# Feed-forward stage of a post-norm transformer layer: the factors of both norms computed in common instructions, second norm's sum and statistics, the low part of x and the output projection in new places

## The chip, the cores and the metric

The kernel runs on one core of one Trainium2 chip. The metric is the device time of one execution in microseconds. The core has five engines that run their own instruction streams in order and meet at semaphores: TensorE (PE, matmuls and transposes; PEld is its weight load), VectorE (DVE), ScalarE (ACT), GpSimd (POOL) and SyncE (SP, which issues the transfers here). A wait at the head of an engine's stream holds everything behind it.

## The reference

8 sequences of 1024 tokens, 256 features, 16 heads of 16, feed-forward width 704, all in float32. A layer is attention, a layer norm over the residual, a feed-forward block whose two linear layers quantize both operands blockwise to a 4-bit grid, and a second layer norm:

```python
def _layernorm(x, axis=-1, eps=1e-05):
    m = jnp.mean(x, axis=axis, keepdims=True)
    v = jnp.var(x, axis=axis, keepdims=True)
    return (x - m) / jnp.sqrt(v + eps)

def fp4_quant_dequant(x):                     # blocks of 16 along the last dim
    xb = x.reshape(shape[:-1] + (shape[-1] // BLOCK, BLOCK))
    scale = jnp.max(jnp.abs(xb), axis=-1, keepdims=True) / 6.0
    scale = jnp.maximum(scale, jnp.float32(1e-12))
    xn = xb / scale
    idx = jnp.searchsorted(_MID, jnp.abs(xn))
    return (_GRID[idx] * jnp.sign(xn) * scale).reshape(shape)

def fp4_linear(x, w):
    return jnp.einsum('bsk,nk->bsn', fp4_quant_dequant(x), fp4_quant_dequant(w))

# attention: softmax(q k^T / 4) v for 16 heads, output projection with scale and bias
x = _layernorm(x + attention(x))              # first norm
h = silu(fp4_linear(x, w_gate)) * fp4_linear(x, w_up)
x = _layernorm(x + fp4_linear(h, w_down))     # second norm
```

## The kernel before

The program has three stages. The first two project q, k and v and compute attention; they end about 1470 us into the profiled execution. The third, `feed`, does everything from the output projection to the second norm. It handles the 8192 tokens as 64 tiles of 128 tokens (tokens on the partitions, features along them) in a software pipeline: in step i each engine does one piece of work for each of several tiles. Tile i-1 is projected and its first norm computed; tile i-2 has x quantized; tile i-3 goes through the gate and up products and silu; tile i-4 has h quantized; tile i-5 has h transposed; tile i-6 goes through the down product; tile i-7 gets residual sum and second norm's statistics; tile i-8 is normalized and stored. The number in the code that goes with each piece is this lag. Steps 1 and 2, and part of step 3, lie inside the attention stage; the steps run to 71. The order of the pieces within a step is written out by hand for each engine, and every hand-over is a semaphore whose count is the tile's number (`due`).

What one step does, engine by engine, with the lines of the profile:

- VectorE: block maxima of h (L1482, 128x44 out) and of x (L1482, 128x16), low part of the transposed x (L1517), the block scales of both in one instruction (L1466) and their reciprocals (L1472), division of x and of h (L1488, 256 and 704 wide), the residual sum y after the output projection (L1537) and its statistics (L1541, L1548), the sum that rounds x (L1495, 256 wide) and the difference that brings it back (L1552), the residual sum z after the down product (L1557), its statistics (L1563, L1573), the sum that rounds h (L1495, 704 wide), and the product silu(gate) * up (L1568).
- GpSimd: the factor of the first norm, (variance + eps) ** -0.5, in two instructions of one column (L1579 the sum, L1580 the power); x's grid value times its scale (L1601); h's difference `hg` (L1608); h's grid value times its scale `hq` (L1613); the factor of the second norm, again L1579 and L1580. In steps 54 to 63 two more instructions at the step's start finish the attention output of that tile (L1589, L1591), because from tile 54 on it is loaded raw.
- ScalarE: copy of the transposed x (L1446), the output (L1375 and L1376 make the bias from mean and factor, L1384 applies both), the two bends of x (L1416, L1420) and of h (L1426, L1430), silu (L1399), three copies of the transposed h (L1407, L1408, L1411), and the first norm (L1375, L1376, L1392).
- TensorE: transposes of x (L1354), output projection (L1286), down product (L1337, whose last, half-height chunk L1345 is done for two tiles at once in every second step), gate and up product (L1298), transposes of h (L1309). In the first step after attention the projection stands ahead of the transposes of x.

The second norm's factor of a step is the last work of that step on GpSimd; the output that ScalarE makes from it is the second piece of the next step. In that next step ScalarE's bends of h (L1426, L1430) stand behind the output, and VectorE's h-rounding sum waits for the second of them (`hm_ready`).

Of the kernel before, what the change touches and what calls it, by code (L numbers as in the profile page):

```python
# [12 lines left out]
ALU = mybir.AluOpType  # L13
# [3 lines left out]
P = 128  # L17
BANK = 512
NB, S, H = 8, 1024, 256
# [1150 lines left out]
def feed(nc, sem, room, first_room, buffers, x_tok, ctx_dram, rden_dram, out_tok, ps, ident, wT, s_all, b_row, wguT, wd, wdT,  # L1170
# [3 lines left out]
    NT = T // P  # L1174
# [9 lines left out]
    def takes(room):  # L1184
# [4 lines left out]
        def take(*shape):  # L1189
# [21 lines left out]
    h = take(I)  # L1211
    hn = take(2, I)
    z = take(2, H)
    names = ("xb_ready ctx_ready wo_psum wo_used mv1_ready rstd1_ready "
             "x1_ready xsum_ready xgrid_ready xq_ready xt_psum xqT_high xqT_ready xn_ready xm_ready xbend_ready hn_ready hm_ready hbend_ready gate_psum up_psum silu_ready h_made "
             "hsum_ready hgrid_ready hq_ready hT_psum hT_ready dn_read dn_psum z_used mv2_ready rstd2_ready fin_ready "
             "stats1_ready stats2_ready grid_chain pow1_chain pow2_chain shift1_chain shift2_chain").split()
    sems = {name: sem(name) for name in names}
    stored = [sem(f"stored{j}") for j in range(2)]

# [6 lines left out]

    def each(ks):
        return (At(None, k, U) for k in ks)

    def sync(sp, ks):
        def load(t):
# [43 lines left out]
    def tensor(pe, ks, cs=range(HC)):  # L1276
# [79 lines left out]
            last.then_inc(sems["xt_psum"], 1)  # L1356

        for i in each(ks):
            order = ((3, x1_by_width), (1, output_projection), (6, down), (3, gate_and_up), (5, h_by_width))
            if i.k == FILL:  # L1360

                pe.wait_ge(wt_split, 2 * HC)
                order = (order[1], order[0]) + order[2:]
            for lag, stage in order:
                if lag == 6 and 0 <= i.k - FILL < IC // 2:
                    wd_across(i.k - FILL)
                if i.plus(-lag).ok(NT):
                    stage(i.plus(-lag))

    def scalar(act, ks, lags=range(9)):  # L1370
# [6 lines left out]
            link.close()  # L1377

        def output(t):
            due(act, "rstd2_ready", t.lin(1, 1))  # L1380
            shift(t, 1, "shift2_chain")

            wait(act, stored[t.slot(2)], t.turn(2, 16))
            nc.scalar.activation(fin[:, t.slot(2)], z[:, t.slot(2)], ACT.Identity, bias=centre[:, 1, 1:2],  # L1384
                                 scale=rstd[:, 1, 1:2]).then_inc(sems["fin_ready"], 1)

        def x1_normal(t):
            due(act, "rstd1_ready", t.lin(1, 1))
            shift(t, 0, "shift1_chain")

            due(act, "z_used", t.lin(1, 1 - U))
            nc.scalar.activation(x1[:, t.slot(U)], y[:, :], ACT.Identity, bias=centre[:, 0, 1:2],  # L1392
                                 scale=rstd[:, 0, 1:2]).then_inc(sems["x1_ready"], 1)
# [53 lines left out]
                                 ACT.Copy).then_inc(sems["xqT_high"], 1)  # L1447

        for i in each(ks):
            for lag, stage in ((3, copy_xqT), (8, output), (2, bend_x), (4, bend_h), (3, silu), (5, copy_hT),  # L1450
                               (1, x1_normal)):
                if lag in lags and i.plus(-lag).ok(NT):
                    stage(i.plus(-lag))
                if lag == 3 and stage is copy_xqT and 0 <= i.k - FILL < IC // 2:
                    copy_wd(i.k - FILL)

    def vector(dve, ks):
# [39 lines left out]
        for i in each(ks):  # L1497
# [12 lines left out]
            if on2:  # L1510
                due(dve, "x1_ready", t2.lin(1, 1))

                due(dve, "xq_ready", t2.lin(1, -1))
                gx.top()
            if on3:
# [4 lines left out]
            if on2 or on4:  # L1520
                which = slice(0 if on4 else NBH, NBH + NBX if on2 else NBH)
                tops, scales, inverses = (blocks[:, i.slot(2), n, which] for n in range(3))
                scale(tops, scales)
                invert(scales, inverses)
            if on2:
                gx.divide().then_inc(sems["xn_ready"], 1)
            if on4:
                gh.divide().then_inc(sems["hn_ready"], 1)
            if on1:
# [7 lines left out]
                nc.vector.scalar_tensor_tensor(out=y[:, :], in0=ps[:, WO, 0:H], scalar=s_all[:, 3:4],  # L1537
                                               in1=pairs[:, pair % PAIRS, 1, half], op0=ALU.mult,
                                               op1=ALU.add).then_inc(sems["wo_used"], 1)
                due(dve, "wo_used", t1.lin(1, 1))  # L1540
                nc.vector.bn_stats(stats[:, 0], y[:, :]).then_inc(sems["stats1_ready"], 1)  # L1541
            if on2:
                gx.add("xm_ready").then_inc(sems["xsum_ready"], 1)
            if on1:

                due(dve, "stats1_ready", t1.lin(1, 1))
                due(dve, "rstd1_ready", t1.lin(1))
                nc.vector.bn_aggr(mv[:, 0], stats[:, 0]).then_inc(sems["mv1_ready"], 1)  # L1548
            if on2:
                due(dve, "xsum_ready", t2.lin(1, 1))  # L1550
                due(dve, "xq_ready", t2.lin(1))
                nc.vector.tensor_tensor(xg[:, :], xn[:, :], xm[:, :],  # L1552
                                        ALU.subtract).then_inc(sems["xgrid_ready"], 1)
            if on7:
                due(dve, "dn_psum", t7.lin(1, 1))
                due(dve, "fin_ready", t7.lin(1, -1))
                nc.vector.tensor_tensor(z[:, t7.slot(2)], ps[:, DN[t7.slot(2)], 0:H], x1[:, t7.slot(U)],  # L1557
                                        ALU.add).then_inc(sems["z_used"], 1)
            if on4:
                gh.add("hm_ready").then_inc(sems["hsum_ready"], 1)  # L1560
            if on7:
                due(dve, "z_used", t7.lin(1, 1))
                nc.vector.bn_stats(stats[:, 1], z[:, t7.slot(2)]).then_inc(sems["stats2_ready"], 1)  # L1563
# [5 lines left out]
            if on7:  # L1569

                due(dve, "stats2_ready", t7.lin(1, 1))
                due(dve, "fin_ready", t7.lin(1))
                nc.vector.bn_aggr(mv[:, 1], stats[:, 1]).then_inc(sems["mv2_ready"], 1)  # L1573

    def gpsimd(pool, ks):
        def power(t, n, chain, name):

            link = Chain(pool, sems[chain], 1, t)
            link(nc.gpsimd.tensor_tensor(rstd[:, n, 0:1], mv[:, n, 1:2], numbers[:, 0:1], ALU.add))  # L1579
            nc.gpsimd.tensor_tensor(rstd[:, n, 1:2], rstd[:, n, 0:1], numbers[:, 1:2],  # L1580
                                    ALU.pow).then_inc(sems[name], 1)
            link.close()

        for i in each(ks):
            if RAW <= i.k < NT:
# [6 lines left out]
            t = i.plus(-1)  # L1592
            if t.ok(NT):
                due(pool, "mv1_ready", t.lin(1, 1))
                due(pool, "x1_ready", t.lin(1))
                power(t, 0, "pow1_chain", "rstd1_ready")
# [21 lines left out]
            if t.ok(NT):  # L1618
# [30 lines left out]
```

## Time and profile before

| | |
|---|---|
| time, median of 3 runs (lowest to highest) | 2056.46 us (2052.69 to 2057.95) |
| time of the profiled execution | 2051.83 us |
| its span | 2050.0 us |
| PE busy | 1987.0 us (97%) |
| DVE busy | 1881.0 us (92%) |
| ACT busy | 1674.6 us (82%) |
| POOL busy | 751.6 us (37%) |
| granted TensorE clock | nine tenths or more of full speed in all 40 slices |
| chain that ended last, by engine | PE 68%, POOL 13%, issue 7%, ACT 7%, DVE 4% |

The span is what the profiler saw of the instructions; 1.8 us lie around it. Busy shares are of the whole span, and about seven tenths of it are projections and attention, which the change leaves as they are. In the chain of waits the shares of POOL come from the lines of `feed` (L1613 and L1608 4% each, L1580 3%, L1601 2%, L1579 1%). A view of a few steps of `feed` says more than any share: the timeline by instruction, in which the same pattern repeats every step.

### The profile page before, as it was taken

The numbers are of one execution on the slowest core, as the hardware profiler recorded it, in microseconds if no ns is written. First come the engines' busy times: TensorE is split into PE (matmuls) and PEld (weight loads), VectorE is DVE, ScalarE is ACT, GpSimd is POOL, SyncE is SP. The second block draws the span as 40 slices with busy tenths as digits, with TensorE's granted clock in tenths as the row PEclk, the third lists the DMA queues.
The fourth block names the chain that finished last, engine by engine and source line by source line (L and its number), as shares of the span: only waits on it lengthen the run. The fifth ranks groups of instructions, "written<-read, shape, count | busy, mean of one in ns | idle before, by whom it ended". The sixth has DMA issues, their size and how long they took to land.

```text
span 2050.0 us, 42089 instructions
## 1 busy us (share of the span) xinstructions
PE 1987.0 (97%) x15806; PEld 1044.0 (51%) x15806; DVE 1881.0 (92%) x2345; ACT 1674.6 (82%) x3244; POOL 751.6 (37%) x749
## 2 busy tenths in 40 slices
PE   8999999999999999999999999999999999999997
PEld 7766333333333333333333333334477777777775
DVE  4788999999999999999999999997399999999996
ACT  6656888888888888888889888888877777777775
POOL 3000446665764561100010010000155555555784
PEclk9999999999999999999999999999999999999999
DMA  7885632444354354435435444542111111111210
GB/s 234 273 248 200 110 51 45 79 96 91 75 100 93 78 95 90 90 82 103 89 71 101 91 84 88 97 91 75 43 40 47 47 40 42 47 47 52 62 32 21
DMA packets 119000, 181.40 MB, mean 88 GB/s; under 512 B 29644, under 2 KB 74444, under 8 KB 118796
## 3 DMA queue, kind: packets, MB, share of 16 engines
q1 hardware_dynamic: 111116, 171.10, 36.2%
q10 hardware_dynamic: 7392, 7.34, 1.1%
q8 instruction: 125, 2.05, 0.5%
q14 instruction: 79, 0.65, 0.1%
q0 software_dynamic: 288, 0.27, 0.1%
HBM read 103.68 MB, written 73.40 MB: 86 GB/s over the span
## 4 chain that ended last, share of the span: by engine, by line
PE 68%; POOL 13%; issue 7%; ACT 7%; DVE 4%; DMA 1%; POOLq 0%; SPq 0%; DVEq 0%
PE ps L913 29%; PE ps L966 28%; POOL hq L1613 4%; PE ps L494 4%; POOL hg L1608 4%; POOL rstd L1580 3%; PE ps L504 3%; ACT craw L1033 2%; PE ps L935 2%; POOL fq L1601 2%; POOL rstd L1579 1%; ACT xm L1420 1%; ACT bend_of_x L1416 1%; PE ps L481 1%; ACT centre L1376 1%
## 5 line engine op out<-in xcount | busy, mean ns | idle before, releaser
L1079 DVE TENSOR_REDUCE negmax<-ps 128x1 f32<-128x1024 f32 x980 | 1182.5, 1219 | 19.7 <-PE ps L913 14.1
L1025 ACT ACTIVATE room<-ps 128x512 f32<-128x512 f32 x2048 | 1102.8, 599 | 118.3 <-PE ps L935 86.7
L935 PE MATMUL ps<-qs,ks 50*128 50x512 f32 x2048 | 745.6, 449 | 1.9 <-ACT room L1025 1.0
L913 PE MATMUL ps<-ks,qs 48*128 48x512 f32 x1960 | 714.5, 444 | 0.0
L966 PE MATMUL ps<-room,vals 128*17 128x256 f32 x8192 | 637.3, 385 | 8.9 <-ACT craw L1033 0.2
L913 PEld LDWEIGHTS ps<-ks,qs 48*128 48x128 f32 x1960 | 288.6, 184 | 414.3 <-DVE negmax L1079 333.0
L164 POOL CAST mrow<-turned_rows 128x32 fp32r<-128x32 f32 x32 | 6.7, 210 | 904.3 <-DVE turned_rows L159 690.8
L966 PEld LDWEIGHTS ps<-room,vals 128*17 128x17 f32 x8192 | 140.0, 95 | 371.4 <-issue 209.5
L935 PEld LDWEIGHTS ps<-qs,ks 50*128 50x128 f32 x2048 | 304.2, 184 | 18.2 <-ACT room L1025 14.3
L1298 PE MATMUL ps<-wguT,xqT 128*128 128x512 f32 (+1 forms) x1152 | 266.8, 384 | 1.4 <-DVE xqT L1517 1.4
L1298 PEld LDWEIGHTS ps<-wguT,xqT 128*128 128x128 f32 x1152 | 210.8, 188 | 48.9 <-issue 9.6
L1337 PE MATMUL ps<-wdT,hT 128*128 128x256 f32 x640 | 150.6, 382 | 5.0 <-ACT hT L1408 5.0
L1136 POOL TENSOR_SCALAR fq<-fq 88x1024 f32<-88x1024 f32 (+1 forms) x42 | 137.5, 3274 | 3.6
L1375 ACT ACTIVATE centre<-mv 128x1 f32<-128x1 f32 x128 | 25.5, 199 | 132.5 <-POOL rstd L1580 132.3
L1337 PEld LDWEIGHTS ps<-wdT,hT 128*128 128x128 f32 x640 | 122.1, 192 | 22.8 <-issue 5.6
L1608 POOL TENSOR_TENSOR hg<-room,hm 128x704 f32<-128x704 f32 x64 | 97.7, 1526 | 45.7 <-DVE room L1495 45.7
L1579 POOL TENSOR_TENSOR rstd<-mv,numbers 128x1 f32<-128x1 f32 x128 | 33.9, 265 | 202.1 <-DVE mv L1548 195.2
L1495 DVE TENSOR_TENSOR room<-room,hm 128x704 f32<-128x704 f32 x64 | 75.6, 1181 | 22.2 <-ACT hm L1430 21.8
L569 ACT ACTIVATE qf<-ps,b_col,s_all 128x512 f32<-128x512 f32 x64 | 49.9, 780 | 52.9 <-PE ps L494 50.0
L1613 POOL TENSOR_TENSOR hq<-hg,blocks 128x704 f32<-128x704 f32 x64 | 88.8, 1388 | 5.0
L494 PE MATMUL ps<-qs,wqk 128*128 128x512 f32 x256 | 80.4, 436 | 0.0
L1138 POOL TENSOR_TENSOR fq<-fq 88x1024 f32<-88x1024 f32 (+1 forms) x36 | 77.3, 2148 | 2.6
(111 smaller groups left out, 2154.3 us busy)
## 6 DMA issues: line engine op xcount, KB each, us to landing
qk_parts<-parts SPq DMA_DIRECT2D x64, 512.0 KB, 3.9
qs<-qk_parts SPq DMA_DIRECT2D x192, 128.0 KB, 4.5
ks<-qk_parts SPq DMA_DIRECT2D x192, 128.0 KB, 7.1
ctx_raw<-craw SPq DMA_DIRECT2D x64, 256.0 KB
ready<-passing SPq DMA_DIRECT2D x27, 512.0 KB, 6.6
pairs<-ready SPq DMA_DIRECT2D x27, 512.0 KB
out_dram<-fin SPq DMA_DIRECT2D x64, 128.0 KB, 1.7
xin<-in_L_attn_x_dram ACTq DMA_DIRECT2D x14, 512.0 KB, 5.5
```

The costliest lines, as they stand in the source:

```text
L494: last = nc.tensor.matmul(ps[:, QK + m % 2, :], wqk[:, a, m // 2, c, (m % 2) * P:(m % 2 + 1) * P], x_half[:, i.slot(2), c, :], start=n == ...
L913: return nc.tensor.matmul(ps[:, MX + 2 * (item[i.k, u] % 2) + bank, :], qs[rows, i.slot(RING), pair, t * P:(t + 1) * P], ks[rows, i.slot(R ...
L935: nc.tensor.matmul(ps[:, score_bank(i, s, n), :], ks[rows, slot, pair, kt * P:(kt + 1) * P], qs[rows, slot, pair, qh * BANK:(qh + 1) * BAN ...
L966: last = nc.tensor.matmul(ps[h * AV:h * AV + DV, PV, cols], vals[:, i.k // NG * KT + kt, i.k % NG * GH + h, :], prob[:, prob_slot(i, s), h ...
L1025: nc.scalar.activation(prob[:, prob_slot(i, s), score_order(i, s)[n], :], ps[:, score_bank(i, s, n), :], ACT.Exp, scale=float(D) ** -0.5). ...
L1079: nc.vector.tensor_reduce(negmax[:, j.slot(RING), max_column(u):max_column(u) + 1], ps[:, bank:bank + 2, :], AX.XY, ALU.max, negate=True). ...
L1136: link(nc.gpsimd.tensor_scalar(dst, norm, mid * mid, gain, ALU.is_gt, ALU.mult))
L1138: link(nc.gpsimd.tensor_tensor(mag, mag, tmp, ALU.add))
L1298: last = nc.tensor.matmul(ps[:, GU + n0 // BANK, 0:n1 - n0], xqT[:, a, c, :], wguT[:, b, c, n0:n1], start=n == 0 and c == 0, stop=n == len ...
L1337: last = nc.tensor.matmul(ps[:, DN[t.slot(2)], 0:H], hT[:, c, :], wdT[:, c, :], start=c == 4, stop=False)
L1608: nc.gpsimd.tensor_tensor(hg[:, :], hn[:, t.slot(2)], hm[:, t.slot(2)], ALU.subtract).then_inc(sems["hgrid_ready"], 1)
L1613: nc.gpsimd.tensor_tensor(hq[:, :].rearrange("p (n e) -> p n e", e=BLK), hg[:, :].rearrange("p (n e) -> p n e", e=BLK), hs[:, t.slot(2), 1 ...
```

## The change

All edits are in `feed`.

1. GpSimd computes the factors of both norms in common instructions of two columns (one of each norm, 128x2), in steps where both norms have a tile; the pair of one-column instructions behind `hq` is gone, and the common pair stands between x's grid value (now first in the step) and h's difference `hg`. It waits for the statistics of both norms. One semaphore, `rstd_ready`, counts the steps in place of one for each norm.
2. VectorE: the block scales and reciprocals stand ahead of the low part of x; the second norm's sum z, statistics and their aggregate stand earlier, between h's division and the first norm's work; the rounding and difference of x stand ahead of y. The first norm's aggregate is last before h's rounding sum.
3. ScalarE: the first norm stands ahead of the copies of the transposed h.
4. TensorE: the output projection stands ahead of the transposes of x in every step.

```diff
 # scalar
-            due(act, "rstd2_ready", t.lin(1, 1))
+            act.wait_ge(sems["rstd_ready"], factors(t.plus(7)))      # output
...
-            due(act, "rstd1_ready", t.lin(1, 1))
+            act.wait_ge(sems["rstd_ready"], factors(t.plus(1)))      # x1_normal
...
-            for lag, stage in ((3, copy_xqT), (8, output), (2, bend_x), (4, bend_h), (3, silu), (5, copy_hT),
-                               (1, x1_normal)):
+            for lag, stage in ((3, copy_xqT), (8, output), (2, bend_x), (4, bend_h), (3, silu), (1, x1_normal),
+                               (5, copy_hT)):
 # tensor
-            order = ((3, x1_by_width), (1, output_projection), (6, down), (3, gate_and_up), (5, h_by_width))
...
+            for lag, stage in ((1, output_projection), (3, x1_by_width), (6, down), (3, gate_and_up), (5, h_by_width)):
 # gpsimd
-        def power(t, n, chain, name):
...
+        def power(i, norms):
...
+            nc.gpsimd.tensor_tensor(rstd[:, norms, 0], mv[:, norms, 1],
+                                    numbers[:, 0:1].to_broadcast([P, norms.stop - norms.start]),
+                                    ALU.add).then_inc(sems["pow_chain"], 1)
+            pool.wait_ge(sems["pow_chain"], i.k)
+            nc.gpsimd.tensor_tensor(rstd[:, norms, 1], rstd[:, norms, 0],
+                                    numbers[:, 1:2].to_broadcast([P, norms.stop - norms.start]),
+                                    ALU.pow).then_inc(sems["rstd_ready"], 1)
...
+            t1, t7 = i.plus(-1), i.plus(-7)
+            if t1.ok(NT):
+                due(pool, "mv1_ready", t1.lin(1, 1))
+                due(pool, "x1_ready", t1.lin(1))
+            if t7.ok(NT):
+                due(pool, "mv2_ready", t7.lin(1, 1))
+                due(pool, "fin_ready", t7.lin(1))
+            if t1.ok(NT) or t7.ok(NT):
+                power(i, slice(0 if t1.ok(NT) else 1, 2 if t7.ok(NT) else 1))
             t = i.plus(-4)
...
-            t = i.plus(-7)
-            if t.ok(NT):
-                due(pool, "mv2_ready", t.lin(1, 1))
-                due(pool, "fin_ready", t.lin(1))
-                power(t, 1, "pow2_chain", "rstd2_ready")
```

`factors(i)` is the number of the step, `i.k`, which is what `rstd_ready` has counted once that step's power is done.

VectorE's order in a step of the steady part, before, from the block scales to h's rounding sum (`room` holds h, hn and z, `fq` holds y, x1, xn and xg):

```order
L1466 SCALAR_TENSOR_TENSOR blocks<-blocks,numbers 128x60
L1472 RECIPROCAL blocks<-blocks 128x60
L1488 SCALAR_TENSOR_TENSOR fq<-fq,blocks 128x256
L1488 SCALAR_TENSOR_TENSOR room<-room,blocks 128x704
L1537 SCALAR_TENSOR_TENSOR fq<-ps,s_all,pairs 128x256
L1541 BN_STATS stats<-fq 128x6
L1495 TENSOR_TENSOR fq<-fq,xm 128x256
L1548 BN_AGGR mv<-stats 128x2
L1552 TENSOR_TENSOR fq<-fq,xm 128x256
L1557 TENSOR_TENSOR room<-ps,fq 128x256
L1495 TENSOR_TENSOR room<-room,hm 128x704
```

The same place in the changed kernel, from the low part of x to h's rounding sum (its lines are other numbers: L1526 is the low part of x, L1492 the divisions, L1536 z, L1499 the rounding sums, L1556 y):

```order
L1526 TENSOR_TENSOR xqT<-ps,xqT 128x256
L1492 SCALAR_TENSOR_TENSOR fq<-fq,blocks 128x256
L1492 SCALAR_TENSOR_TENSOR room<-room,blocks 128x704
L1536 TENSOR_TENSOR room<-ps,fq 128x256
L1499 TENSOR_TENSOR fq<-fq,xm 128x256
L1542 BN_STATS stats<-room 128x6
L1546 TENSOR_TENSOR fq<-fq,xm 128x256
L1556 SCALAR_TENSOR_TENSOR fq<-ps,s_all,pairs 128x256
L1563 BN_AGGR mv<-stats 128x2
L1566 BN_STATS stats<-fq 128x6
L1570 BN_AGGR mv<-stats 128x2
L1499 TENSOR_TENSOR room<-room,hm 128x704
```

The low part of x came from ahead of the scales to behind the reciprocals, the statistics of z came from behind h's rounding sum to ahead of it, and the first norm's aggregate went from the middle to the last place before that sum.

GpSimd's order, before, one step from the first norm's factor to the second norm's:

```order
L1579 TENSOR_TENSOR rstd<-mv,numbers 128x1
L1580 TENSOR_TENSOR rstd<-rstd,numbers 128x1
L1601 TENSOR_TENSOR fq<-fq,blocks 128x256
L1608 TENSOR_TENSOR hg<-room,hm 128x704
L1613 TENSOR_TENSOR hq<-hg,blocks 128x704
L1579 TENSOR_TENSOR rstd<-mv,numbers 128x1
L1580 TENSOR_TENSOR rstd<-rstd,numbers 128x1
```

And in the changed kernel, one step:

```order
L1603 TENSOR_TENSOR fq<-fq,blocks 128x256
L1583 TENSOR_TENSOR rstd<-mv,numbers 128x2
L1587 TENSOR_TENSOR rstd<-rstd,numbers 128x2
L1619 TENSOR_TENSOR hg<-room,hm 128x704
L1624 TENSOR_TENSOR hq<-hg,blocks 128x704
```

Four small instructions became two with two columns, and they stand right ahead of h's difference; nothing is behind `hq` in the step any more.

## Rows read from the trace of the kernel before

**Rows 1.** Waits, 1480 to 1950 us: who waited for whom, total, times, longest.

```profile
ACT centre L1375 <- POOL rstd L1580: 102.2, 50, 2.2
...
DVE room L1495 <- ACT hm L1430: 17.4, 48, 0.4
```

**Rows 2.** Timeline of one step: start, duration, instruction, idle before and its releaser.

```profile
1708.88 1.30 DVE L1495 TENSOR_TENSOR room<-room,hm 128x704 f32<-128x704 f32 x1 [0.38 <-ACT hm L1430]
...
1710.26 1.53 POOL L1608 TENSOR_TENSOR hg<-room,hm 128x704 f32<-128x704 f32 x1 [0.82 <-DVE room L1495]
...
1711.87 1.39 POOL L1613 TENSOR_TENSOR hq<-hg,blocks 128x704 f32<-128x704 f32 x1
...
1713.21 0.19 POOL L1579 TENSOR_TENSOR rstd<-mv,numbers 128x1 f32<-128x1 f32 x1
...
1713.48 0.55 POOL L1580 TENSOR_TENSOR rstd<-rstd,numbers 128x1 f32<-128x1 f32 x1
...
1714.07 0.20 ACT L1375 ACTIVATE centre<-mv 128x1 f32<-128x1 f32 x1 [2.18 <-POOL rstd L1580]
...
1714.65 0.60 ACT L1384 ACTIVATE fin<-room,centre,rstd 128x256 f32<-128x256 f32 x1
...
1716.01 0.78 ACT L1426 ACTIVATE bend_of_h<-room 128x704 f32<-128x704 f32 x1
...
1717.73 1.30 DVE L1495 TENSOR_TENSOR room<-room,hm 128x704 f32<-128x704 f32 x1 [0.38 <-ACT hm L1430]
```

**Rows 3.** Timeline, VectorE in the same step, from the product to the divisions.

```profile
1710.44 0.86 DVE L1568 TENSOR_TENSOR room<-room,ps 128x704 f32<-128x704 f32 x1
...
1711.34 0.89 DVE L1482 TENSOR_REDUCE blocks<-room 128x44 f32<-128x704 f32 x1
...
1712.14 0.41 DVE L1482 TENSOR_REDUCE blocks<-fq 128x16 f32<-128x256 f32 x1
1712.47 0.41 DVE L1517 TENSOR_TENSOR xqT<-ps,xqT 128x256 fp32r<-128x256 f32 x1
1712.80 0.53 DVE L1466 SCALAR_TENSOR_TENSOR blocks<-blocks,numbers 128x60 f32<-128x60 f32 x1
...
1713.37 0.53 DVE L1472 RECIPROCAL blocks<-blocks 128x60 f32<-128x60 f32 x1
...
1713.93 0.42 DVE L1488 SCALAR_TENSOR_TENSOR fq<-fq,blocks 128x256 f32<-128x256 f32 x1
...
1714.27 0.88 DVE L1488 SCALAR_TENSOR_TENSOR room<-room,blocks 128x704 f32<-128x704 f32 x1
```

**Rows 4.** Timeline, the end of the same step on VectorE and GpSimd.

```profile
1715.08 0.48 DVE L1537 SCALAR_TENSOR_TENSOR fq<-ps,s_all,pairs 128x256 f32<-128x256 f32 x1
...
1716.47 0.17 DVE L1548 BATCH_NORM_AGGREGATE mv<-stats 128x2 f32<-128x6 f32 x1
1716.59 0.42 DVE L1552 TENSOR_TENSOR fq<-fq,xm 128x256 f32<-128x256 f32 x1
1716.73 0.34 POOL L1579 TENSOR_TENSOR rstd<-mv,numbers 128x1 f32<-128x1 f32 x1 [2.69 <-DVE mv L1548]
...
1717.66 0.62 POOL L1601 TENSOR_TENSOR fq<-fq,blocks 128x256 f32<-128x256 f32 x1
```

**Rows 5.** Timeline, h's rounding sum in two steps without a second norm.

```profile
1489.63 0.89 DVE L1495 TENSOR_TENSOR room<-room,hm 128x704 f32<-128x704 f32 x1 [0.18 <-ACT hm L1430]
...
1497.68 0.89 DVE L1495 TENSOR_TENSOR room<-room,hm 128x704 f32<-128x704 f32 x1 [0.19 <-ACT hm L1430]
```

**Rows 6.** Timeline, a step of the raw tiles: GpSimd's extra work beside h's division.

```profile
1960.98 0.94 POOL L1589 TENSOR_TENSOR pairs<-pairs 128x256 f32<-128x256 f32 x1
...
1961.25 1.42 DVE L1488 SCALAR_TENSOR_TENSOR room<-room,blocks 128x704 f32<-128x704 f32 x1
...
1961.88 1.40 POOL L1591 TENSOR_TENSOR pairs<-pairs,b_row 128x256 f32<-128x256 f32 x1
```

**Rows 7.** Windows: busy PE, PEld, DVE, ACT, POOL (x instructions), clock, DMA share, GB/s.

```profile
1700.00:1800.00 100.00, 94.41 (x479) 78.23 (x478) 93.51 (x192) 73.34 (x174) 58.04 (x80) 1.00 0.15 47
```

More of the change, by code:

```diff
@@ L1213, in feed @@
     z = take(2, H)
-    names = ("xb_ready ctx_ready wo_psum wo_used mv1_ready rstd1_ready "
+    names = ("xb_ready ctx_ready wo_psum wo_used mv1_ready rstd_ready "
              "x1_ready xsum_ready xgrid_ready xq_ready xt_psum xqT_high xqT_ready xn_ready xm_ready xbend_ready hn_ready hm_ready hbend_ready gate_psum up_psum silu_ready h_made "
-             "hsum_ready hgrid_ready hq_ready hT_psum hT_ready dn_read dn_psum z_used mv2_ready rstd2_ready fin_ready "
-             "stats1_ready stats2_ready grid_chain pow1_chain pow2_chain shift1_chain shift2_chain").split()
+             "hsum_ready hgrid_ready hq_ready hT_psum hT_ready dn_read dn_psum z_used mv2_ready fin_ready "
+             "stats1_ready stats2_ready grid_chain pow_chain shift1_chain shift2_chain").split()
     sems = {name: sem(name) for name in names}
@@ L1229, in each, with factors @@
         return (At(None, k, U) for k in ks)
+    def factors(i):
+        return i.k
     def sync(sp, ks):
@@ L1358, in tensor @@
         for i in each(ks):
-            order = ((3, x1_by_width), (1, output_projection), (6, down), (3, gate_and_up), (5, h_by_width))
             if i.k == FILL:
                 pe.wait_ge(wt_split, 2 * HC)
-                order = (order[1], order[0]) + order[2:]
-            for lag, stage in order:
+            for lag, stage in ((1, output_projection), (3, x1_by_width), (6, down), (3, gate_and_up), (5, h_by_width)):
                 if lag == 6 and 0 <= i.k - FILL < IC // 2:
@@ L1514, in vector @@
                 gx.top()
+            if on2 or on4:
+                which = slice(0 if on4 else NBH, NBH + NBX if on2 else NBH)
+                tops, scales, inverses = (blocks[:, i.slot(2), n, which] for n in range(3))
+                scale(tops, scales)
+                invert(scales, inverses)
             if on3:
@@ L1519, in vector @@
                                         ALU.subtract).then_inc(sems["xqT_ready"], 1)
[L1520 to L1524, printed above, removed]
             if on2:
@@ L1528, in vector @@
                 gh.divide().then_inc(sems["hn_ready"], 1)
+            if on7:
+                due(dve, "dn_psum", t7.lin(1, 1))
+                due(dve, "fin_ready", t7.lin(1, -1))
+                nc.vector.tensor_tensor(z[:, t7.slot(2)], ps[:, DN[t7.slot(2)], 0:H], x1[:, t7.slot(U)],
+                                        ALU.add).then_inc(sems["z_used"], 1)
+            if on2:
+                gx.add("xm_ready").then_inc(sems["xsum_ready"], 1)
+            if on7:
+                due(dve, "z_used", t7.lin(1, 1))
+                nc.vector.bn_stats(stats[:, 1], z[:, t7.slot(2)]).then_inc(sems["stats2_ready"], 1)
+            if on2:
+                due(dve, "xsum_ready", t2.lin(1, 1))
+                due(dve, "xq_ready", t2.lin(1))
+                nc.vector.tensor_tensor(xg[:, :], xn[:, :], xm[:, :],
+                                        ALU.subtract).then_inc(sems["xgrid_ready"], 1)
             if on1:
@@ L1539, in vector @@
                                                op1=ALU.add).then_inc(sems["wo_used"], 1)
+            if on7:
+                due(dve, "stats2_ready", t7.lin(1, 1))
+                due(dve, "fin_ready", t7.lin(1))
+                nc.vector.bn_aggr(mv[:, 1], stats[:, 1]).then_inc(sems["mv2_ready"], 1)
+            if on1:
                 due(dve, "wo_used", t1.lin(1, 1))
                 nc.vector.bn_stats(stats[:, 0], y[:, :]).then_inc(sems["stats1_ready"], 1)
-            if on2:
-                gx.add("xm_ready").then_inc(sems["xsum_ready"], 1)
-            if on1:
                 due(dve, "stats1_ready", t1.lin(1, 1))
-                due(dve, "rstd1_ready", t1.lin(1))
+                wait(dve, sems["rstd_ready"], factors(i.plus(-1)))
                 nc.vector.bn_aggr(mv[:, 0], stats[:, 0]).then_inc(sems["mv1_ready"], 1)
[L1549 to L1558, printed above, removed]
             if on4:
                 gh.add("hm_ready").then_inc(sems["hsum_ready"], 1)
-            if on7:
-                due(dve, "z_used", t7.lin(1, 1))
-                nc.vector.bn_stats(stats[:, 1], z[:, t7.slot(2)]).then_inc(sems["stats2_ready"], 1)
             if on3:
@@ L1568, in vector @@
                 nc.vector.tensor_tensor(h[:, :], sg[:, :], up, ALU.mult).then_inc(sems["h_made"], 1)
[L1569 to L1573, printed above, removed]
     def gpsimd(pool, ks):
-        def power(t, n, chain, name):
[L1578 to L1582, printed above, removed]
+        def power(i, norms):
[6 more added lines that the diff above has]
+                                    ALU.pow).then_inc(sems["rstd_ready"], 1)
         for i in each(ks):
@@ L1591, in gpsimd @@
                 nc.gpsimd.tensor_tensor(with_b, with_b, b_row[:, 1], ALU.add).then_inc(sems["xb_ready"], 1)
-            t = i.plus(-1)
-            if t.ok(NT):
-                due(pool, "mv1_ready", t.lin(1, 1))
-                due(pool, "x1_ready", t.lin(1))
-                power(t, 0, "pow1_chain", "rstd1_ready")
             t = i.plus(-2)
@@ L1616, in gpsimd @@
                                         ALU.mult).then_inc(sems["hq_ready"], 1)
-            t = i.plus(-7)
-            if t.ok(NT):
-                due(pool, "mv2_ready", t.lin(1, 1))
-                due(pool, "fin_ready", t.lin(1))
-                power(t, 1, "pow2_chain", "rstd2_ready")
     return Programs(sync, gpsimd, tensor, scalar, vector)
```

## The prediction

> **What bounds the kernel now.** I read the page first, then the waits of ScalarE, VectorE and TensorE in the steady part of `feed`, then the timeline of one step, and last short pieces where a step is different (the first steps, and the raw tiles). The page's busy shares point at TensorE and VectorE, and the shares of its chain at TensorE, but most of the span is attention, so neither says what a step of `feed` is waiting for. The waits do: ScalarE stands idle for 102.2 us in 50 steps, up to 2.2 us each, ahead of L1375 for the power L1580, and VectorE stands idle 0.4 us ahead of L1495 for ScalarE's `hm` in 48 steps [rows 1].
>
> In the timeline these two are parts of one loop that closes after one step [rows 2]. Start to start: h's rounding sum on VectorE to `hg` 1.38, `hg` to `hq` 1.61, `hq` to the second norm's factor 1.34, its two instructions and the hand-over to ScalarE 0.86 (0.27 and 0.59), the bias and the output, then the bends of x up to the first bend of h 1.94 (0.58 and 1.36), that bend and `hm` to the next rounding sum 1.72. Together 8.85 us, and 1708.88 to 1717.73 is 8.85. Nothing in it depends on the output itself; the bends of h only stand behind it in ScalarE's stream. So the second norm's factor sets the step, and the change takes it away from there. The question is what the next loop is, and how long.
>
> **The next loop in the old kernel.** Steps without a second norm show it: rounding sum to rounding sum is 8.05 there [rows 5]. Its links can be read in the steady step. VectorE's block scales L1466 start at 1712.80 and end at 1713.33, just after `hq` ends at 1713.26 [rows 2, 3]. No semaphore ties them; the two engines exclude each other. The same is seen at the other places where a VectorE instruction with two inputs in SBUF meets a GpSimd instruction: the rounding sum takes 1.30 beside x's grid value (1717.66 to 1718.28) and 0.89 where it is alone [rows 2, 4, 5]; the factor's sum L1579 takes 0.34 beside x's difference and 0.19 alone, and ends 0.06 after the other [rows 2, 4]; h's division takes 1.42 in place of 0.88 beside L1589 [rows 3, 6]. The loser ends its own length less some 0.14 after the holder. So `hq` holds back the scales, these the reciprocals, these the divisions, these the bends, and these the rounding sum, whose result makes the next `hg`.
>
> **The change, part by part.**
>
> *Second factor out from behind `hq`.* The loop of 8.85 is cut: the output in the next step finds its factor long done. ScalarE's idle 2.2 us go.
>
> *Common factors ahead of `hg`.* They wait for the first norm's aggregate, and that now starts 0.12 ahead of the rounding sum, which is what an aggregate takes from VectorE's stream (1716.47 to 1716.59). GpSimd follows an aggregate's start after 0.26 [rows 4], so 0.14 after the rounding sum has begun, and by the rows above it is held until that ends. In us after the rounding sum's start: sum of the factor ends at 0.89 + 0.06 = 0.95; power starts at 1.03 (0.08 behind, as 1713.40 to 1713.48) and ends at 1.58; `hg`, which no longer waits for anything else, starts 0.05 before that end, as L1579 does behind `hq`, at 1.53 [rows 2]. Queued behind this wait are `hg`, `hq` and everything that hangs on them. Against 1.38 now this adds 0.15.
>
> *The power on two columns.* No row shows it. The power on one column takes 0.55 where the sum on the same shape takes 0.19 [rows 2]. If the difference of 0.36 is paid once, the second column costs nothing; if it is paid for each column, it costs 0.36 a step. The trace can't say which; I take the middle, 0.18, and keep both ends. Below nothing it cannot go, as the work of one column is in it. The Trainium skill (GPSIMD Engine Reference, Elementwise, side-by-side cycle accounting) gives about 2.6 cycles an element at 1.2 GHz; by that a second column would be 2 ns, and the sum below would lose its whole term for it. That page speaks of ordinary arithmetic, and the power's 0.36 us for one element a partition is far off that rate, so no run here shows what it does for a second.
>
> *VectorE's order.* I space its instructions as the rows do: the next starts 0.08 before the end if independent, 0.03 after it if it reads the result [rows 3]. From `hq` to the reciprocals 1.50 as now (1711.87 to 1713.37), if the scales still lose to `hq`. Then the low part of x in between, 0.45, to x's division 0.33, to h's division 0.34. That is 1.12 where there was 0.90 (1713.37 to 1714.27). From h's division on, up to the rounding sum: 0.81 to z, 0.34 to x's rounding sum, 0.34 to z's statistics, 0.33 to x's difference, 0.34 to y, 0.40 to the second aggregate, 0.11 to the first statistics, 0.46 to the first aggregate (it reads them), 0.12. Together 3.25 (0.42 for the 256-wide instructions, 0.48 for y, from rows 3 and 4). ScalarE would have `hm` ready after 0.96 + 1.72 = 2.68 [rows 2, 3], so VectorE itself closes the loop, and all that was moved ahead of the rounding sum counts in full.
>
> *The new loop.* 1.53 + 1.61 + 1.50 + 1.12 + 3.25 = 9.01 with a free second column, 9.19 with 0.18. It is longer than the 8.85 that it replaces.
>
> *Do the scales still lose?* They follow x's block maxima, and those now wait for x1. From the power's end: 0.04 to ScalarE, 0.23 and 0.35 for the bias, 0.60 for x1, 0.03, 0.44 for the maxima: 1.69. `hq` starts 0.05 before that end plus 1.61: at 1.56. So the scales come 0.13 us late and wait for the whole of `hq`. The power's length moves both alike.
>
> *Moves that cost nothing by themselves.* The copies of the transposed h now follow x1 and come late, some 3.9 us after the rounding sum, and the down product behind them. The projection that now stands ahead of the transposes fills that wait. TensorE is busy 94.41 of 100 us [rows 7], so its own work is 0.944 x 8.85 = 8.35 a step, and below 9.0 it has room; h's product may wait for the up product, and is then up to 0.7 us late, but between it and the end of `hq` VectorE has more slack than that. If that cover is gone, it is the term of the second rival.
>
> *Raw tiles, 10 steps.* GpSimd's two extra instructions now come right behind `hq`, where VectorE has scales and divisions. L1591 holds x's division back by about 0.33: it ends near 1.36 after `hq`, the division would have begun at 0.89 and ends 0.28 after the holder. In the old kernel the like delay (1.42 for 0.88) was covered by ScalarE's output [rows 6].
>
> **Sum.** Steps 8 to 53: 46 x (9.01 - 8.85) = 7.4. Raw steps: 10 x (0.16 + 0.33) = 4.9. First steps without second norm: without z and its statistics VectorE needs some 0.2 less, 8.8 against 8.05, three times: 2.2. Last steps without x: a loop about 0.3 shorter than now, two or three times: -0.7. Second column: 58 x 0.18 = 10.4. Together 24, so 2051.8 + 24 = 2076 for a profiled execution. The median shown is 4.6 above the profiled one; by it, 2080. I say 2079.
>
> **Rivals.**
>
> *A, the port falls the other way and the factors cost nothing* (chance 0.20). If GpSimd's small instructions run beside the rounding sum, `hg` starts at about 0.97 with a free column or 1.10 with 0.18; the loop is 8.45 or 8.58, close to TensorE's own 8.35. 46 x -0.27 = -12, raw steps about 0, ends +1: 2040 to 2046. For it: the removed wait is real, 2 us a step. Against it: L1579 is held by just such an instruction in every step [rows 4].
>
> *B, the scales slip in between `hg` and `hq`* (0.12). The margin is 0.13 us. Then `hq` starts some 0.1 late and x's division waits for its end: 1.71 + 1.71 + 1.39 + 0.20 + 3.25 = 8.26. But then the down product behind the late copies, with its tail in every second step, delays h's product by more than 1 us, and the scales miss in the step after. Half the steps 8.35 to 8.5 and half 9.19 give about 8.85: no gain, raw steps +3: 2051 to 2060.
>
> *C, the second column costs a full 0.36 or more* is the upper end of the forecast: 14 + 21 = 35, so 2087 to 2092.
>
> **How the numbers follow.** Forecast 0.68, A 0.20, B 0.12. A change below 0.3% (6 us) cannot be told from none here; so faster 0.20, same 0.12, slower 0.68. The likeliest case has 2066 (free column) to 2092 (0.36) as its own range. For 8 in 10 I take 2048 to 2096: above to a column somewhat dearer than 0.36, below through B and the nearer edge of A.
>
> **What the new profile would show.** ScalarE's wait ahead of L1375 for the power behind `hq` is gone, and it now waits ahead of the first norm. The factor's sum on two columns takes about 0.75, ending just after the rounding sum's end; `hg` starts 1.5 to 1.9 after the rounding sum's start. VectorE shows no wait for `hm`; the scales take over 1 us, ending with `hq`. Rounding sums come 9.0 to 9.4 apart. I am wrong if the factor's sum takes 0.2 and `hg` starts within 1.2 (A), or if the scales take 0.3 in many steps (B), or if steps are under 8.8.

## The result, and the profile after

| | before | changed |
|---|---|---|
| median (lowest to highest) | 2057.2 us (2052.69 to 2059.94) | 2074.12 us (2069.46 to 2077.52) |
| runs | 4 | 4 |
| profiled execution, span | 2051.83, 2050.0 | 2069.46, 2067.6 |

The ratio is 1.0083, 95% interval 1.0056 to 1.011: slower by 17 us, and the whole interval lies above the 0.3% (6 us) under which two kernels can't be told apart here. The forecast was 2079, slower.

The page of the changed kernel, busy time by engine and the chain that ended last:

```profile
span 2067.6 us, 41973 instructions
...
PE 1987.8 (96%) x15806; PEld 1037.9 (50%) x15806; DVE 1890.5 (91%) x2345; ACT 1685.8 (82%) x3244; POOL 728.7 (35%) x633
...
PE 79%; DVE 10%; issue 4%; ACT 4%; POOL 2%; DMA 0%; DVEq 0%; SPq 0%; POOLq 0%; ACTq 0%
```

No engine has more instructions than before, GpSimd has fewer (633 for 749), and the kernel is slower. The chain has moved from GpSimd (13% before, 2% now) to TensorE (68% to 79%), which would make TensorE the suspect; the experiments below ask that.

The waits of the changed kernel between 1480 and 1950 us, of ScalarE, VectorE and TensorE (who waited for whom, total, times, longest):

```profile
ACT centre L1379 <- POOL rstd L1587: 40.4, 51, 1.6
ACT room L1403 <- PE ps L1304: 39.0, 51, 1.6
...
DVE room L1577 <- PE ps L1304: 23.4, 28, 1.7
DVE blocks L1486 <- ACT fq L1396: 5.6, 24, 0.3
...
PE ps L1360 <- ACT hT L1412: 35.8, 51, 1.6
```

The wait of [rows 1] for the factor behind `hq` is gone. What L1379 now waits for is the factors ahead of `hg`, in front of the first norm. VectorE no longer waits for `hm` ahead of its rounding sum. New waits of ScalarE and VectorE stand on TensorE's gate and up products (L1304): together 62.4 us now, 1.7 before. TensorE's wait for the copies of the transposed h, which now come late, is not new but has grown, from 20.0 us in 49 times to 35.8 in 51.

One step of the steady part in the timeline of the changed kernel (start, duration, instruction), only the links that close it:

```profile
1705.39 0.18 DVE L1570 BATCH_NORM_AGGREGATE mv<-stats 128x2 f32<-128x6 f32 x1
1705.49 0.86 DVE L1499 TENSOR_TENSOR room<-room,hm 128x704 f32<-128x704 f32 x1
1705.65 0.75 POOL L1583 TENSOR_TENSOR rstd<-mv,numbers 128x2 f32<-128x2 f32 x1 [0.45 <-DVE mv L1570]
...
1706.48 0.69 POOL L1587 TENSOR_TENSOR rstd<-rstd,numbers 128x2 f32<-128x2 f32 x1
...
1707.13 1.53 POOL L1619 TENSOR_TENSOR hg<-room,hm 128x704 f32<-128x704 f32 x1
...
1708.73 1.39 POOL L1624 TENSOR_TENSOR hq<-hg,blocks 128x704 f32<-128x704 f32 x1
...
1709.37 0.83 DVE L1470 SCALAR_TENSOR_TENSOR blocks<-blocks,numbers 128x60 f32<-128x60 f32 x1
...
1710.23 0.53 DVE L1476 RECIPROCAL blocks<-blocks 128x60 f32<-128x60 f32 x1
1710.67 0.36 DVE L1526 TENSOR_TENSOR xqT<-ps,xqT 128x256 fp32r<-128x256 f32 x1
1710.95 0.41 DVE L1492 SCALAR_TENSOR_TENSOR fq<-fq,blocks 128x256 f32<-128x256 f32 x1
...
1711.28 0.89 DVE L1492 SCALAR_TENSOR_TENSOR room<-room,blocks 128x704 f32<-128x704 f32 x1
...
1714.49 0.86 DVE L1499 TENSOR_TENSOR room<-room,hm 128x704 f32<-128x704 f32 x1
```

The rounding sum starts 0.10 behind the first norm's aggregate; the factors' sum follows 0.16 later, takes 0.75 and ends 0.05 after the rounding sum. `hg` starts 1.64 after the rounding sum, `hq` 1.60 later, the reciprocals 1.50 after `hq`, x's division 0.72 and h's division 1.05 after them, the next rounding sum 3.21 after that: 9.00. That is the loop that stands where the 8.85 of [rows 2] stood. Every second step is 9.11: it holds TensorE's tail, the half-height last chunk of the down product for two tiles at once, and z waits 0.11 for it.

What made this loop long can be read beside the first steps of the kernel before, where the same loop closes at 8.05 [rows 5]:

```profile
1490.96 1.52 POOL L1608 TENSOR_TENSOR hg<-room,hm 128x704 f32<-128x704 f32 x1
...
1492.57 1.39 POOL L1613 TENSOR_TENSOR hq<-hg,blocks 128x704 f32<-128x704 f32 x1
...
1494.06 0.53 DVE L1472 RECIPROCAL blocks<-blocks 128x60 f32<-128x60 f32 x1
...
1494.97 0.88 DVE L1488 SCALAR_TENSOR_TENSOR room<-room,blocks 128x704 f32<-128x704 f32 x1
```

From the rounding sum at 1489.63 to the next at 1497.68 the links are 1.33, 1.61, 1.49, 0.91 and 2.71. In the changed kernel they are 1.64, 1.60, 1.50, 1.05 and 3.21. The common factors put in 0.31, the low part of x 0.14, and 0.50 came in between h's division and the rounding sum, where z, its statistics and its aggregate now stand and the wait for `hm` (0.19) is gone. Together 0.95.

Where the 17.6 us of the two spans lie, by the starts of h's 64 rounding sums: up to the first -2.0; the first three steps after it +2.5; the 46 steady ones, 9.06 in the mean against 8.83, +10.4; the ten with raw tiles, 9.41 against 8.79, +6.2; the last four +1.6; what follows the last rounding sum -1.0. That is 17.7, and 0.1 of it is rounding.

### The profile page after: what moved, and what is told of

It is laid out like the page before. It is cut to its first block, busy times and chain, and to the rows that moved or that the text cites. A ratio compares the mean times of both kernels' runs of the same rounds, so it can differ in the third digit from the quotient of the medians.

```text
span 2067.6 us, 41973 instructions
## 1 busy us (share of the span) xinstructions
PE 1987.8 (96%) x15806; PEld 1037.9 (50%) x15806; DVE 1890.5 (91%) x2345; ACT 1685.8 (82%) x3244; POOL 728.7 (35%) x633
## 4 chain that ended last, share of the span: by engine, by line
PE 79%; DVE 10%; issue 4%; ACT 4%; POOL 2%; DMA 0%; DVEq 0%; SPq 0%; POOLq 0%; ACTq 0%
PE ps L913 29%; PE ps L966 28%; PE ps L1304 7%; PE ps L494 4%; PE ps L1343 4%; PE ps L504 3%; ACT craw L1033 2%; PE ps L935 2%; DVE room L1577 1%; DVE blocks L1470 1%; POOL rstd L1583 1%; DVE room L1492 1%; POOL rstd L1587 1%; PE ps L1351 1%; PE ps L481 1%
## 5 line engine op out<-in xcount | busy, mean ns | idle before, releaser
L1304 PE MATMUL ps<-wguT,xqT 128*128 128x512 f32 (+1 forms) x1152 | 266.6, 385 | 4.0 <-DVE xqT L1526 4.0
L1304 PEld LDWEIGHTS ps<-wguT,xqT 128*128 128x128 f32 x1152 | 210.7, 189 | 53.3 <-issue 10.3
L1603 POOL TENSOR_TENSOR fq<-fq,blocks 128x256 f32<-128x256 f32 x64 | 40.5, 632 | 239.1 <-DVE fq L1546 239.1
L1343 PEld LDWEIGHTS ps<-wdT,hT 128*128 128x128 f32 x640 | 116.0, 191 | 17.2 <-issue 2.3
L1403 ACT ACTIVATE room<-ps 128x704 f32<-128x704 f32 x64 | 48.5, 757 | 47.9 <-PE ps L1304 47.9
L1577 DVE TENSOR_TENSOR room<-room,ps 128x704 f32<-128x704 f32 x64 | 56.8, 887 | 29.7 <-PE ps L1304 29.4
```

The source lines that it names most:

```text
L1304: last = nc.tensor.matmul(ps[:, GU + n0 // BANK, 0:n1 - n0], xqT[:, a, c, :], wguT[:, b, c, n0:n1], start=n == 0 and c == 0, stop=n == len ...
L1343: last = nc.tensor.matmul(ps[:, DN[t.slot(2)], 0:H], hT[:, c, :], wdT[:, c, :], start=c == 4, stop=False)
```

## The experiments

Theory 1: a step is closed by VectorE and GpSimd alone, as in the sum of the prediction. Theory 2, which the page's chain suggests: TensorE closes it, through the late copies, the down product, the up product and h's product. Each kernel is the changed one with the edit shown; ratios are to the kernel before.

### The low part of x back ahead of the scales

```diff
+            if on3: ...   # low part of x (L1526), moved up again
             if on2 or on4: ...   # scales, reciprocals
-            if on3: ...
```

> The changed kernel with the low part of x back ahead of the block scales on VectorE; all else as changed. Theory 1 (the step is closed by VectorE and GpSimd alone: rounding sum, factors, hg, hq, scales held back by hq, reciprocals, divisions, rounding sum): the low part now fits into the time in which VectorE waits for hq anyway, and from the reciprocals' start to x's division it is 0.56 as before instead of 0.72, so a step takes about 8.90 instead of 9.06 and the kernel 8 to 10 us less, about 2065. Theory 2 (TensorE closes the step: late copies of the transposed h, down product, gate and up product, h's product): the low part only gets earlier than TensorE needs it, no change within 3 us, 2074.

Measured: 2071.5 us, ratio 1.0064 (1.0042 to 1.0085). The steps are 8.90 and 9.11 in turn. The steps without a tail gain 0.10 (9.00 to 8.90); those with a tail gain nothing, and the timeline of such a step shows the first reason:

```profile
1703.45 0.39 ACT L1450 ACTIVATE xqT<-ps 128x256 fp32r<-128x256 f32 x1
...
1703.87 0.42 DVE L1521 TENSOR_TENSOR xqT<-ps,xqT 128x256 fp32r<-128x256 f32 x1 [1.00 <-ACT xqT L1450]
...
1704.21 0.21 DVE L1470 SCALAR_TENSOR_TENSOR blocks<-blocks,numbers 128x60 f32<-128x60 f32 x1
```

The low part waits 1.00 for ScalarE's copy, which waits for the transposes behind the late copies, and comes off after `hq` has ended (1702.78 + 1.39 = 1704.17). The reciprocals start 1.68 after `hq` and no longer 1.50, which uses up the 0.16; in the steps without a tail the wait is 0.35 and they start at 1.54. The second reason is the tail: z starts 6.70 after the rounding sum in the steps of 9.11, here as in the changed kernel, right behind the tail's end at 6.67. So theory 1 missed a wait here (2065 expected), and TensorE's side lies just under the loop in one kind of step and holds the other. The medians of this run and of the next are too close to the changed kernel's to be told from it (the intervals of the ratios overlap); it is the steps that tell. The last row gives the hold of the port in one number: with `hq` over, the scales take 0.21; beside it up to 1.34.

### The copies back ahead of the first norm

```diff
-            ... (3, silu), (1, x1_normal), (5, copy_hT)):
+            ... (3, silu), (5, copy_hT), (1, x1_normal)):
```

> The changed kernel with ScalarE's three copies of the transposed h back ahead of the first norm. The copies then start some 2 us earlier in the step and end before the factors are there. Theory 1: only the small wait of z for TensorE's tail in every second step goes (0.11 in 9.11), so 0 to 4 us less, 2070 to 2074. Theory 2: TensorE's chain starts 2 us earlier, and with it the step gets shorter until TensorE's own work of 8.35 bounds it: 20 us less or more, 2055 or below.

Measured: 2073.41 us, ratio 1.007 (1.0047 to 1.0093). All steps are 9.00. The copies come 1.7 earlier and TensorE's transposes of x and down product 1.3, TensorE stands idle for the low part of x instead (36.7 us in 50 waits), and nothing is gained but the 0.11 of every second step. Theory 2 has fallen for the changed kernel as it is: TensorE sets no more than that 0.11.

### Both at once

> The changed kernel with both single edits at once: the low part of x ahead of the block scales, and the copies of the transposed h ahead of the first norm. In the run with the low part alone every second step kept 9.11, because the low part then waited for the transposes of x, which stand behind the late copies (1.00 and 0.35 on VectorE). Theory 1 with that addition: with the copies early nothing holds the low part, and all steps fall to 9.00 less the 0.16 between reciprocals and x's division, 8.84 to 8.86: 10 to 14 us below the changed kernel, 2060 to 2064, still above the kernel before. Rival (the loop over the port is not what closes the step): no more than either edit alone, 2070 or more.

Measured: 2061.25 us (10 runs), ratio 1.0027 (1.0013 to 1.0041). All steps are 8.85. Alone the two edits gave 2.6 and 0.7 us of their medians, no more than noise, together 12.9: the gain of the low part had been hiding behind the late copies, and the sum of theory 1 holds once the low part has nothing to wait for.

### The factors apart in the same place

```diff
-            ... one sum and one power of [P, 2]
+            for n in range(norms.start, norms.stop):
+                ... sum of [P, 1], wait, power of [P, 1]
```

> The changed kernel with the factors of the two norms computed in the same place of GpSimd's stream, but in two pairs of one-column instructions instead of one pair of two columns. Theory 1: all of GpSimd's time between the rounding sum and hg is on the loop; the second pair adds 0.08 + 0.19 + 0.08 + 0.55, less the 0.14 that the second column costs, so 0.6 to 0.75 a step and 35 to 43 us, about 2112. Rival (the common form is what costs, the place is free): the time falls or stays at 2074 or less.

Measured: 2115.52 us, ratio 1.0273 (1.0246 to 1.0299). Steps of 9.64 and 9.75, 0.64 more. What lies between the rounding sum and `hg` on GpSimd counts in full, and the common form is the cheap part of the change: it saves 0.64 a step against two pairs in that place.

### The projection back behind the transposes

```diff
-            ... ((1, output_projection), (3, x1_by_width), (6, down), ...):
+            ... ((3, x1_by_width), (1, output_projection), (6, down), ...):
```

> The changed kernel with the output projection back behind the transposes of x on TensorE. Theory 1: the projection no longer fills the wait for the late copies, so the down product starts 0.87 later, and with it the tail for which z waits and the up product for which h's product waits; the steps with a tail grow from 9.11 by up to 0.8, the others little: 0 to 20 us more, most likely about 2082. Rival (TensorE has the room anyway): 2074 within 3.

Measured: 2095.79 us, ratio 1.0194 (1.0168 to 1.022). Steps of 9.00 and 9.97 in turn. In a step with a tail z stands 0.92 for it:

```profile
1701.27 0.70 PE L1351 MATMUL ps<-wdT,hT 64*128 64x256 f32 x4
...
1702.00 0.42 DVE L1536 TENSOR_TENSOR room<-ps,fq 128x256 f32<-128x256 f32 x1 [0.92 <-PE ps L1351]
```

The direction was as expected, the size a little above the upper end (22 us for 0 to 20; 9.97 is 0.86 more for up to 0.8). So this part of the change was needed by the others: the copies behind the first norm make TensorE late, and the projection fills that gap. With the projection in front the late copies cost 0.7 us against early ones, which is nothing clear of noise; with the projection behind, the kernel with late copies is 22 us slower. A kernel with early copies and the projection behind was not run.

### The common factors, but early

VectorE's order in a step, with the common factors ahead of x's grid value on GpSimd:

```diff
-  h's and x's maxima, scales, reciprocals, low part, division of x, of h, z, x's sum, z's statistics,
-  x's difference, y, second aggregate, y's statistics, first aggregate, h's rounding sum, product
+  h's and x's maxima, y, low part, y's statistics, scales, reciprocals, first aggregate, z, division of x,
+  of h, z's statistics, x's sum, second aggregate, x's difference, h's rounding sum, product
```

> The changed kernel with the common factors kept, but earlier: VectorE takes y ahead of the low part of x, the first norm's statistics and aggregate around the scales, z and its statistics around the divisions, and the second aggregate ahead of x's difference; GpSimd computes the factors ahead of x's grid value. ScalarE and TensorE as changed. Theory 1: the factors' sum no longer stands behind the rounding sum at the shared port, and both instructions fit into GpSimd's idle time; hg follows the rounding sum after 0.97 to 1.4 instead of 1.64, and divisions to rounding sum shrink from 3.2 to about 2.7. The step falls to 8.4 to 8.6, close to TensorE's own 8.35: 2036 to 2050, below both kernels. Rival (the two-column instructions or the common wait themselves cost the time): stays at 2065 or above.

Measured: 2042.71 us, ratio 0.9925 (0.9901 to 0.995). Faster than both. Steps are 8.27 and 8.87 in turn. The factors' sum takes 0.20, as the rounding sum no longer stands ahead of it; h's rounding sum waits for `hm` again (38.9 us in 55 waits), and z for the tail (13.1 us in 26 waits).

### The same with z behind h's division

> The early version (2042.7) with z one place later, behind h's division instead of between the aggregate and x's division. There z stood on the way from hq to the bends of h (0.30 a step) and waited for TensorE's tail in every second step (0.5 and more), 8.27 and 8.87. If that wait holds the loop, the steps come to TensorE's own work, 8.35 to 8.5 in the mean instead of 8.57: 4 to 12 us less, 2031 to 2039. Rival: TensorE's tail and the up product behind it are what is late, and then only another instruction waits: 2043 within 3.

Measured: 2030.52 us (2027.04 to 2031.78), ratio 0.9875 (0.9853 to 0.9897), the fastest here: 25.7 us below the kernel before, 43.6 below the changed one. Steps of 8.05 and 8.65. Its timeline, from the scales to `hg`:

```profile
1700.34 0.20 DVE L1470 SCALAR_TENSOR_TENSOR blocks<-blocks,numbers 128x60 f32<-128x60 f32 x1
...
1700.57 0.53 DVE L1476 RECIPROCAL blocks<-blocks 128x60 f32<-128x60 f32 x1
...
1701.48 0.88 DVE L1492 SCALAR_TENSOR_TENSOR room<-room,blocks 128x704 f32<-128x704 f32 x1
...
1703.81 0.20 POOL L1583 TENSOR_TENSOR rstd<-mv,numbers 128x2 f32<-128x2 f32 x1 [3.95 <-DVE mv L1565]
...
1704.08 0.69 POOL L1587 TENSOR_TENSOR rstd<-rstd,numbers 128x2 f32<-128x2 f32 x1
1704.18 0.89 DVE L1499 TENSOR_TENSOR room<-room,hm 128x704 f32<-128x704 f32 x1 [0.24 <-ACT hm L1434]
...
1704.73 0.82 POOL L1612 TENSOR_TENSOR fq<-fq,blocks 128x256 f32<-128x256 f32 x1
...
1705.52 1.53 POOL L1619 TENSOR_TENSOR hg<-room,hm 128x704 f32<-128x704 f32 x1
```

Both factor instructions start ahead of the rounding sum, division to rounding sum is 2.70 instead of 3.21, and TensorE is the engine that is full:

```profile
1500.00:1900.00 400.00, 396.37 (x2015) 326.51 (x2015) 363.41 (x812) 310.74 (x716) 218.53 (x240) 1.00 0.16 49
```

396.37 of 400 us against 368.84 in the same stretch of the changed kernel. Busy time a step comes to 8.27 here and to 8.35 in the changed kernel, near the 8.35 that the prediction gave as TensorE's own work [rows 7], so a mean step of 8.35 leaves TensorE hardly any room. The steps of 8.05 have the links of the loop in the old kernel's first steps: 1.34, 1.60, 1.50, 0.91 and 2.70 in the one that begins at 1704.18. In those of 8.65 h's product waits some 0.8 for TensorE's up product (21.3 us in 28 waits, L1304), the scales come 1.87 after `hq`, and TensorE closes the step. The time was 0.5 below the range that was expected.

### The factors where the change put them, VectorE shorter

VectorE's order: maxima, y, low part, y's statistics, scales, reciprocals, divisions, z, x's sum, first aggregate, x's difference, z's statistics, second aggregate, rounding sum, product; the copies ahead of the first norm; GpSimd as changed.

> The changed kernel with y and the low part of x ahead of the scales, z, x's sum, first aggregate, x's difference, z's statistics and second aggregate behind h's division, the copies ahead of the first norm, and the common factors where the change put them (behind x's grid value, ahead of hg). The second aggregate then comes right ahead of the rounding sum, as the first did in the changed kernel, and the factors' sum is held by it again (hg 1.64 behind the rounding sum), but VectorE has three instructions less between hq and the rounding sum: hq to rounding sum 1.50 + 0.56 + 0.34 + about 2.7, and 3.24 ahead of it, 8.35 to 8.5 a step. Theory 1: 2036 to 2046. If the place of the factors alone decides: 2065 or more.

Measured: 2032.64 us, ratio 0.9887 (0.9866 to 0.9908), 3 us below what was expected. All steps are 8.39.

```profile
1701.98 0.18 DVE L1570 BATCH_NORM_AGGREGATE mv<-stats 128x2 f32<-128x6 f32 x1
...
1702.31 0.89 DVE L1499 TENSOR_TENSOR room<-room,hm 128x704 f32<-128x704 f32 x1
1702.39 0.86 POOL L1583 TENSOR_TENSOR rstd<-mv,numbers 128x2 f32<-128x2 f32 x1
...
1703.98 1.52 POOL L1619 TENSOR_TENSOR hg<-room,hm 128x704 f32<-128x704 f32 x1
```

Here the factors' sum is held by the rounding sum as in the changed kernel (0.86), and `hg` starts 1.67 after it, and still the step is 0.66 shorter than the changed kernel's mean. So the place of the factors in GpSimd's stream isn't what makes the changed kernel slow by itself. It takes both: the 1.64 there and the 0.72 and 3.21 on VectorE. With 0.56 and 2.71 there, the 1.67 can be borne: TensorE is busy 396.48 of 400 us here too, so a shorter loop would have gained little more. The copies were moved as well; by the run with the copies alone, and by that with both edits, they are worth 0.06 a step and the freeing of the low part.

## Why the prediction was right

*The bound and the next loop.* Right. The wait for the second factor went, and the loop through the port that the first steps showed [rows 5] took its place.

*Common factors ahead of `hg`.* Right in mechanism and nearly in size: the factors' sum was to end 0.95 after the rounding sum's start and ended at 0.91; `hg` was to start at 1.53 with a free second column or 1.71 with 0.18, and starts at 1.64.

*Second column.* The one term that no row showed. The power on two columns takes 690 ns in the mean, on one 551: 0.14, between the ends 0 and 0.36 and near the value taken. The Trainium skill (GPSIMD Engine Reference, Elementwise — side-by-side cycle accounting) gives about 2.6 cycles an element for a two-input addition, which by an estimate from it is 2 ns for a second column. The trace does not carry that over to the power: it shows 0.14 us.

*VectorE's order.* 1.50, 0.72 (forecast 0.78), 0.33 (0.34) and 3.21 (3.25): the low part takes 0.36 here and not 0.41. Division to rounding sum is VectorE's own time, as forecast, without a wait for `hm`; in the steps with a tail z's wait adds 0.11 to it, which the forecast did not have.

*The scales still lose.* Right that they lose, and in every second step by nearly the 0.13 forecast. In the step shown they started 0.64 after `hq`, as h's product came late (the wait for L1304); in the step after 0.12:

```profile
1717.73 1.39 POOL L1624 TENSOR_TENSOR hq<-hg,blocks 128x704 f32<-128x704 f32 x1
...
1717.85 1.34 DVE L1470 SCALAR_TENSOR_TENSOR blocks<-blocks,numbers 128x60 f32<-128x60 f32 x1
```

They take 0.83 and 1.34 and end 0.07 to 0.08 after `hq`. Rivals A and B did not come about, and of C's 0.36 there were 0.14.

*Moves that cost nothing.* Half right. TensorE's side had room, but less than I gave it: z waits 0.11 for the tail in every second step, which I had not seen, and 22 us hang on the projection's new place. h's product does wait for the up product, up to 0.85 in the steps without a tail (forecast: up to 0.7), and the slack ahead of `hq`'s end covers it, as forecast.

*Raw tiles.* Forecast +0.49 a step against 8.85, and 0.18 for the second column; measured 9.41 against 8.79, so +0.62 for 0.67. L1598 holds x's division, which takes 0.82 for 0.41, as worked out:

```profile
1946.88 0.73 POOL L1598 TENSOR_TENSOR pairs<-pairs,b_row 128x256 f32<-128x256 f32 x1
...
1947.07 0.82 DVE L1492 SCALAR_TENSOR_TENSOR fq<-fq,blocks 128x256 f32<-128x256 f32 x1
```

*The sum.* 24 forecast, 17.6 between the profiled executions, 17 between the medians. The steady steps make most of the difference: 46 x (9.19 - 8.85) = 15.6 forecast, 10.4 measured. A step without a tail is 9.00, 0.19 less than forecast: 0.07 up to `hg` (of it 0.04 the second column), 0.06 at the low part, 0.05 from x's division to the rounding sum, and 0.01 up to `hq`. A step with a tail gives 0.11 of that back. The two ends were less well understood. The first steps were to cost 2.2; they cost 2.5 less the 2.0 by which the first rounding sum comes earlier. The last steps were to gain 0.7 and lost 0.5 in all (1.6 less 1.0). These two errors have opposite signs and nearly cancel, which is luck, but they are small beside the 17.

## What to carry to other kernels

When a wait closes a loop of 8.85 and the loop behind it is 8.05, look at what the new order puts into the second one before counting the 0.8 as won: here 0.95 came into it. Steps that lack a part (here the first of the pipeline) show the second loop in the old trace. Statistics and small factors belong into the time in which an engine waits anyway, ahead of the division here, not between it and the sum that everyone waits for; and moves that hide behind one another are to be tried together, since two that are worth nothing clear of noise alone gave 13 us as a pair.

## What the runs showed of the hardware

A power of a second column on GpSimd costs 0.14 us beyond the 0.55 of the first, while 704 columns of a product cost 1.39 in all.

A VectorE instruction of 0.21 us that starts 0.12 behind a GpSimd instruction of 1.39 takes 1.34. The Trainium skill (SBUF — State Buffer, SBUF: two separate sides) says that of a GpSimd instruction and a VectorE instruction with two inputs in SBUF the one that starts first gets the shared port pair for its whole length and the other blocks. The trace agrees with that for `hq`, for x's grid value and for the two instructions of the raw tiles, but not for the power, which is long for its one or two columns:

```profile
1489.58 0.55 POOL L1580 TENSOR_TENSOR rstd<-rstd,numbers 128x1 f32<-128x1 f32 x1
```

In the kernel before the rounding sum starts at 1489.63 [rows 5], 0.05 into this power, and takes 0.89; if it were held until the power's end it would take about 1.25, an estimate from where it ends beside x's grid value, 0.75 behind that one's end [rows 2, 4]. With two columns it is the same: in the fastest run above the power runs from 1704.08 to 1704.77, and the rounding sum that starts at 1704.18 takes 0.89. So the power's 0.55 or 0.69 costs GpSimd's own time and not VectorE's.

The time that a held instruction stands is counted as busy. The scales, at 0.21 of work, show up to 1.1 us more on VectorE, and no view of waits lists it; the reciprocals start 1.50 after `hq` whether the scales are recorded with 0.53, 0.83 or 1.34.
